# Transposing loads of ATT1 and Y3SP made in larger pieces, in a two-layer transformer kernel

## The reference

```python
x = layernorm(x + quat_attention(x))        # layer 0: 16 heads, full attention over 4096 tokens
x = layernorm(x + quantised_linear(x))      # blocks of 32 rounded to an fp6 grid, both operands
x = layernorm(x + window_attention(x))      # layer 1: q 16 heads, k and v 2 heads, window 256
                                            # out @ Wo + bo
xr = mu_r*x + (1-mu_r)*x_prev;  xk = mu_k*x + (1-mu_k)*x_prev     # x_prev: the token before
x = layernorm(x + sigmoid(xr @ W_r.T) * (relu(xk @ W_k.T)**2 @ W_v.T))
```

## Time and profile before

| | us |
|---|---|
| median of the runs shown (2 runs, 5682.71 to 5690.19) | 5686.45 |
| the profiled execution, its own time | 5682.38 |
| its span, from first to last instruction, slowest core (core 4) | 5680.8 |
| span of the fastest core (core 1) | 5646.2 |
| TensorE busy, share of the span | 2773.3 (49%) |
| ScalarE busy | 1807.1 (32%) |
| VectorE busy | 1534.1 (27%) |
| mean granted TensorE clock, share of full speed | 0.646 |

### The profile page before, as it was taken

How to read it: one execution, slowest core, us unless ns; L and a number is a source line. 1 busy time by engine, 2 the same in 40 slices (tenths; PEclk the granted TensorE clock), 3 DMA queues, 4 the chain that set the end, 5 groups by cost and what they waited for, 6 DMA issues and landing times.

```text
span 5680.8 us, 63040 instructions; the slowest of 8 cores (5646.2 to 5680.8 us)
## 1 busy us (share of the span) xinstructions
PE 2773.3 (49%) x17810; PEld 1397.2 (25%) x17810; DVE 1534.1 (27%) x3379; ACT 1807.1 (32%) x2292; POOL 177.8 (3%) x339
## 2 busy tenths in 40 slices
PE   0265257777775234555555555532445454104534
PEld 0122114444442122232323232311222222001112
DVE  0345310000001133413131313151333333013544
ACT  0122007778770133354444444410222222001000
POOL 0011010000001000000000000000000000000000
PEclk9966576666667555656666666666556555557766
DMA  1321230000003200000000000013000000101000
GB/s 15 75 36 28 45 45 4 4 1 4 4 4 48 52 12 20 13 10 16 10 16 11 16 11 16 11 28 70 25 27 22 25 25 27 40 20 27 18 30 23
DMA packets 200268, 132.74 MB, mean 23 GB/s; under 512 B 130152, under 2 KB 181008, under 8 KB 199952
## 3 DMA queue, kind: packets, MB, share of 16 engines
q0 software_dynamic: 46864, 59.31, 5.9%
q1 hardware_dynamic: 153088, 69.41, 4.4%
HBM read 117.63 MB, written 28.31 MB: 26 GB/s over the span
## 4 chain that ended last, share of the span: by engine, by line
PE 33%; ACT 22%; DVE 16%; DMA 9%; issue 9%; SPq 8%; POOL 1%; DVEq 1%; ACTq 1%; PEldq 0%; POOLq 0%
ACT TE L521 17%; PE PALL L551 9%; PE PALL L509 4%; SPq L1320 3%; PE PALL L464 3%; PE PALL L332 2%; SPq L1086 2%; PE PALL L1256 2%; PE PALL L1104 2%; PE PALL L797 2%; DMA TY<-XFF 2%; PE PALL L1188 1%; PE PALL L1463 1%; PE PALL L1403 1%; DMA SMALL<-QBI 1%
## 5 line engine op out<-in xcount | busy, mean ns | idle before, releaser
L521 ACT ACTIVATE TE<-PALL,BIASB 128x768 bf16<-128x768 f32 x1536 | 1383.5, 901 | 965.1 <-PE PALL L509 586.2
L509 PE MATMUL PALL<-TY 64*128 64x384 bf16 x3072 | 863.8, 423 | 697.7 <-ACT TE L521 685.8
L509 PEld LDWEIGHTS PALL<-TY 64*128 64x128 bf16 x3072 | 299.0, 97 | 1208.1 <-issue 1129.0
L551 PE MATMUL PALL<-TY,TE 128*128 128x65 bf16 x9216 | 530.5, 243 | 0.0
L551 PEld LDWEIGHTS PALL<-TY,TE 128*128 128x128 bf16 x9216 | 503.4, 131 | 60.3 <-issue 60.3
L558 DVE RECIPROCAL SMALL<-PALL 128x6 f32<-128x6 f32 x48 | 9.4, 196 | 1643.6 <-PE PALL L551 1617.0
L332 PE MATMUL PALL<-TY,TE 128*128 128x512 bf16 (+1 forms) x832 | 230.4, 450 | 362.1 <-DVE TE L298 210.9
L1232 ACT ACTIVATE TE<-PALL,BIASB 128x256 bf16<-128x256 f32 (+2 forms) x240 | 154.6, 644 | 464.5 <-PE PALL L1217 444.6
L464 PE MATMUL PALL<-TE,TY 128*128 128x512 bf16 x512 | 149.0, 444 | 239.8 <-DMA TY<-XFF 239.8
L1104 PE MATMUL PALL<-TE,TY 128*128 128x512 bf16 x288 | 102.9, 522 | 238.0 <-DMA TY<-ATT 236.9
L332 PEld LDWEIGHTS PALL<-TY,TE 128*128 128x128 bf16 x832 | 93.0, 114 | 499.3 <-issue 475.1
(11 more groups left out here) (171 smaller groups left out, 2628.1 us busy)
## 6 DMA issues: line engine op xcount, KB each, us to landing
TY<-XFF POOLq DMA_DIRECT2D x192, 128.0 KB, 4.7
TY<-XST POOLq DMA_DIRECT2D x18, 512.0 KB, 3.7
YOUT<-TE SPq DMA_DIRECT2D x18, 512.0 KB, 2.6
ATT<-TY SPq DMA_DIRECT2D x36, 128.0 KB, 1.8
TY<-ATT SPq DMA_TRANSPOSE x288, 2.3
Y2SP<-TY SPq DMA_DIRECT2D x18, 256.0 KB, 2.0
TE<-Y2SP POOLq DMA_DIRECT2D x18, 256.0 KB, 2.9
ATT<-TY SPq DMA_DIRECT2D x18, 256.0 KB, 2.3
```

What stands on the lines that cost most here:

```text
L509: t.matmul(o_, l_, r_, start=True, stop=True, tile_position=tp)),
L521: ss.activation(o_, i_, AF.Exp, bias=BIASB[:, 63:64], scale=0.125)),
L551: t.matmul(o_, l_, r_, start=s0, stop=False, skip_group_check=True)),
```

## The change

Two sets of transposing loads are issued in larger pieces. The same bytes go to the same engines.

1. `p4_slice` loads ATT1 by query tile: at slices 0, 3, 6, ... it issues 8 loads of 384 rows by 128 columns; the two slices after it read their part of the same buffer. The two `AF1` buffers grow from 2 KB to 6 KB per partition each, and the two `Y3B` buffers move behind them. The 18 sets of 8 loads become 6 sets of 8: 48 for 144.
2. The reload of Y3SP goes in five groups of 512, 512, 512, 512 and 256 rows: 40 loads for 144. Each group waits until the spills of its rows have landed, and for the group two before. What reads `Y3C` waits for the group that holds its columns.

```diff
@@ -1057,33 +1057,39 @@
         l_b1o = sch.dma("g", "dgm", lambda g: g.dma_start(out=ROWR[0:1, 0:1024], in_=B1O),
                         waits=[t_fbrow, tp2_nop, p2v_last])
 
-        def AF1(p, c):
-            base = p * 1024
-            return TY2.bitcast(BF16)[:, base + c * 128: base + c * 128 + 128]
+        def AF1(p, c, a, n):
+            base = p * 3072
+            return TY2.bitcast(BF16)[:, base + c * QT + a: base + c * QT + a + n]
 
         def Y3B(p):
-            return TY2.bitcast(BF16)[:, 2048 + p * 1024: 2048 + p * 1024 + 1024]
+            return TY2.bitcast(BF16)[:, 6144 + p * 1024: 6144 + p * 1024 + 1024]
 
         Z3AP = TEV(12288, F32, 1024)
         JUNK3 = TEV(16384, F32, 1024)
 
-        p4s = {"oproj": {}, "z3": {}, "spill": {}, "n": 0}
+        p4s = {"oproj": {}, "z3": {}, "spill": {}, "af1": {}, "n": 0}
 
         def p4_slice(sl):
             p = sl % 2
-            tldA = None
-            for c in range(8):
-                w = []
-                if c == 0:
-                    w = [("dsp", sch.cnt["dsp"])]
-                    if p4s["oproj"].get(sl - 2):
-                        w.append(p4s["oproj"][sl - 2])
-                    if sl < 2:
-                        w += [tp2_nop, p2v_last]
-                tldA = sch.dma("y", "dw2" if p == 0 else "dw3",
-                               (lambda y, s_=ATT1[128 * sl:128 * sl + 128,
-                                                  128 * c:128 * c + 128],
-                                d_=AF1(p, c): y.dma_start_transpose(d_, s_)), waits=w)
+            g = sl // 3
+            pg = g % 2
+            if sl % 3 == 0:
+                tldA = None
+                for c in range(8):
+                    w = []
+                    if c == 0:
+                        w = [("dsp", sch.cnt["dsp"])]
+                        if p4s["oproj"].get(3 * (g - 2) + 2):
+                            w.append(p4s["oproj"][3 * (g - 2) + 2])
+                        if g < 2:
+                            w += [tp2_nop, p2v_last]
+                    tldA = sch.dma("y", "dw2" if pg == 0 else "dw3",
+                                   (lambda y, s_=ATT1[QT * g:QT * g + QT,
+                                                      128 * c:128 * c + 128],
+                                    d_=AF1(pg, c, 0, QT): y.dma_start_transpose(d_, s_)),
+                                   waits=w)
+                p4s["af1"][g] = tldA
+            tldA = p4s["af1"][g]
             wy = [p4s["z3"][sl - 2]] if sl >= 2 else [("dy2", 16 * NSL), p2v_last]
             ldy2 = sch.dma("g", "dx0" if p == 0 else "dx1",
                            (lambda g, d_=TEV(20480 + p * 2048, BF16, 1024),
@@ -1099,7 +1105,7 @@
                         if psum_free.get(bank):
                             w.append(psum_free[bank])
                     sch.op("t", (lambda t, o_=PB(bank, 0, 512),
-                                 l_=AF1(p, ic),
+                                 l_=AF1(pg, ic, (sl % 3) * 128, 128),
                                  r_=TEV(24576, BF16, 8 * D)[:, ic * D + nh * 512: ic * D + nh * 512 + 512],
                                  s0=(ic == 0): t.matmul(o_, l_, r_, start=s0, stop=False)),
                            waits=w)
@@ -1304,21 +1310,21 @@
         tp3_nop = sch.op("t", lambda t: t.nop(), mark=True)
 
         zc = sch.op("v", lambda v: v.memset(SMALL[:, 166:167], 0.0))
-        rl_tok = {}
-        for sl in range(NSL):
-            dl = "dl0" if sl % 2 == 0 else "dl1"
+        RLG = [(0, 512), (512, 512), (1024, 512), (1536, 512), (2048, 256)]
+        rl_grp = {}
+        for gi, (a0, ng) in enumerate(RLG):
+            dl = "dl0" if gi % 2 == 0 else "dl1"
             tok = None
             for c in range(8):
                 w = []
                 if c == 0:
-                    w = [("dy3", 16 * (sl + 1)), tp3_nop, st1["pv_norm"]]
-                    if sl >= 2:
-                        w.append(rl_tok[sl - 2])
-                tok = sch.dma("y", dl, (lambda y, d_=Y3C(c, 128 * sl, 128),
-                                        s_=Y3SP[128 * sl:128 * sl + 128,
-                                                128 * c:128 * c + 128]:
+                    w = [("dy3", 16 * ((a0 + ng) // 128)), tp3_nop, st1["pv_norm"]]
+                    if gi >= 2:
+                        w.append(rl_grp[gi - 2])
+                tok = sch.dma("y", dl, (lambda y, d_=Y3C(c, a0, ng),
+                                        s_=Y3SP[a0:a0 + ng, 128 * c:128 * c + 128]:
                                         y.dma_start_transpose(d_, s_)), waits=w)
-            rl_tok[sl] = tok
+            rl_grp[gi] = tok
 
         if stage == "p4":
             for sl in range(NSL):
@@ -1346,16 +1352,14 @@
         TILES = [(0, 512), (512, 512), (1024, 512), (1536, 512), (2048, 256)]
 
         def rl_need(ti):
-            a, n = TILES[ti]
-            m = (a + n - 1) // 128
-            return [rl_tok[m], rl_tok[m - 1]]
+            return [rl_grp[ti]] + ([rl_grp[ti - 1]] if ti >= 1 else [])
         stash_tok = None
         for ti in range(1, 5):
             a = TILES[ti][0]
             for c in range(8):
                 stash_tok = sch.op("v", (lambda v, d_=SMALL[:, 96 + (ti - 1) * 8 + c: 97 + (ti - 1) * 8 + c],
                                          s_=Y3C(c, a - 1, 1): v.tensor_copy(d_, s_)),
-                                   waits=[rl_tok[(a - 1) // 128]] if c == 0 else [])
+                                   waits=[rl_grp[ti - 1]] if c == 0 else [])
         r_done = None
         xr_free = None
         for ti, (a, n) in enumerate(TILES):
```

## The result

The kernel after takes 5435.25 us (median of 9 runs, 5426.63 to 5464.16), the kernel before 5682.91 us beside it (8 runs). The ratio is 0.957, 95% interval 0.955 to 0.9591. The profiled execution took 5440.6 us; its slowest core is core 6.

A forecast was written before the change was run, and what follows sets the result against it. The prediction took SyncE's issuing of transposing loads as the bound. Savings of 125.0 us in the reload and 126.2 in the slices, 251 us together, took the median 5686.45 to 5435 us, range 5415 to 5462, chance 0.85.

The forecast's parts named there:

- SyncE's issues set both places: Reload and slices: the issue of transposing loads, not their transfer, is the limit; 1.290 us per issue in the reload.
- The price of an issue: Transposing loads: 1.262 us for 512 rows plus 0.058 us of gap, 1.32 us; eight of 384 rows 10.20 us.
- the hold-up: First group of the reload, beside the load of WRT: 8 us of delay, with 0.5 and 11.4 as ends.
- The bound that the prediction worked out for the first group: Reload's first group: 15.9 us of DMA work, begun 2 us in, so it lasts at most about 18 us.
- The spill distance: Slices: from one spill to the next, 6.3 us of VectorE's chain in place of a mean of 24.55.
- The rival of the clock: Second slice: TensorE does not get its upper clock level, 16 us of gain lost, 5451 us; chance 0.05.
- The slices as a whole: Slices: seven spill distances shorter by 18.25 us, 127.7 us, less 1.5 us for larger loads, saving 126.2 us.
- The reload was taken right: Reload: 40 issues, 52.8 us, plus 8 us of delay make 60.8 us for 185.8, saving 125.0 us.
- bytes, not issues: Reload and slices: a transposing load takes time in proportion to its rows; 5682 us, no change; chance 0.03.
- Contention that does not end with WRT: Reload: each of the five groups takes 21.98 us, the reload 110 us, the kernel 5484 us; chance 0.05.
- The slower rival: Large issues on the path, 88 of them: each held for 6.37 us, 5879 us, slower by 3.4%; chance 0.02.
- a later stage that grows: Sign of being wrong: a later stage grows, such as the feed-forward part, from L1367 to the end 601 us.

The follow-up runs named there:

- e1: The kernel before with only the reload of Y3SP made in groups of 512 rows, the slices loading ATT1 by 128 rows; 5557.55 us, ratio 0.9769.
- e2: The kernel before with only the slices loading ATT1 by 384 rows, the reload staying at 144 issues; 5580.6 us, ratio 0.9809.
- e4: The kernel after with the load of WRT held back until the last group of the reload has landed; 5437.97 us, ratio 0.9561.
- e3: The kernel after with the reload in nine groups of 256 rows, 72 issues for 40; 5479.52 us, ratio 0.9659.
- e5: The kernel after with the reload in three groups of 768 rows, 24 issues for 40; 5425.27 us, ratio 0.9527.

## Why the prediction was right

The forecast was 5435 us, and the measurement 5435.25. The gain was forecast at 251 us, from a kernel before at 5686.45; it is 247.7 us, from 5682.91 beside it. The mechanism holds, and the last few microseconds of agreement are luck, as said below. Its terms:

- That SyncE's issues set both places: e1 and e2 show it one by one, and the parts add up as the prediction took them to.
- The price of an issue by the earlier trace rows: 1.261 us for 512 rows and 10.18 us for eight of 384. The reload was to take 60.8 us and takes 60.71 on core 6, the first group 18 us and takes 18.9, the others 10.5 each and take 10.45. e4 shows that the cause of the hold-up is WRT, which the prediction could only take from one likeness, and 9 us for it from first to last issue on core 4.
- The size of the hold-up is a choice that came out well: 8 us, taken between 0.5 and 11.4. The bound that the prediction worked out for the first group, about 18 us from 11.8 us of weights and 4.1 us of transposes, did not hold: the first group takes 17.0 to 19.7 us on the eight cores, over 18 on four of them. In the 22 us from 4753 on core 6 the weight queue kept the engines busy for 61.5% of the time, 13.5 us, and the queue of the transposes for 37.1%, 8.2 us for 11 loads: side by side both took more of the engines than in the rows that the bound was taken from (a transposing load 0.75 us in place of 4.1 / 8 = 0.51).
- The spill distance: 6.3 us forecast, 6.37 measured, VectorE's chain as said. The rival of the clock is out: 1.90 us for eight matmuls in the second slice.
- The slices as a whole were taken 4 us too high: 126.2 forecast, 122.5 measured. Compared on core 6 in both kernels, the first two spills of a tile lie closer by 18.4 us, but the ATT1 loads of that tile and the next by only 17.5 (136.2 us apart, before 153.7). The stretch from the query load to the next ATT1 load got 0.8 us longer (104.7 for 103.9). Part of it is in the rows above: the query projection takes 12.84 us, and TensorE had stood 19.65 us before it. The same row of the kernel before, on core 6:

```profile
4093.55 12.28 PE L1188 MATMUL PALL<-TY 128*128 128x384 bf16 x64 [17.88 <-DMA TY<-Y2SP]
```

That the longer stand causes the slower start is what it looks like; no run varied it alone.
- The reload was taken right to 0.1 us in the stage table (125.0 forecast, 124.9 measured). So the exact total is luck: the 4 us too many in the slices are made up by the kernel before, which came out 3.5 us lower than the median that the forecast started from. Two figures of the prediction are off and change nothing: without hold-up the time is 5435 - 8 = 5427 us, not 5425, and with the price going by the bytes it is 5435 + 125 + 124 = 5684, not 5682.

The rival "bytes, not issues" falls with e3. "Contention that does not end with WRT" falls with the four later groups, 10.45 us each beside a DMA share of 0.40. The slower rival, every issue at 6.4 us, has its grain of truth: in every traced reload by 512 rows with WRT beside it the longest issue of each core takes 4.4 to 7.1 us, and in e4, with WRT held back, none takes over 1.27.

The rule that sequencer time is usually small relative to the DMA itself (the Trainium skill, DMA: Bandwidth & Descriptors, "Issuing engines are not separate DMA queues") would have had this change bring nothing. These runs disagree, with 1.23 us of SyncE for a load that keeps the DMA engines busy for 0.12 of that time.

The last stage of the kernel after is 3 us longer than before in the mean. The prediction had named a later stage that grows as a sign of being wrong (601 us from L1367 to the end); on core 6 that is 621.5 us, from 4817.47. It is cores 6 and 7 alone, at a lower granted clock; the windows of core 6 and of core 0 over it:

```profile
5000.00:5439.00 439.00, 201.80 (x772) 84.50 (x782) 211.25 (x396) 30.30 (x73) 0.00 (x0) 0.61 0.06 22
```

```profile
5000.00:5418.50 418.50, 176.60 (x772) 75.51 (x784) 211.28 (x396) 30.31 (x73) 0.00 (x0) 0.69 0.06 23
```

Core 6 had 427.7 us in this stage before, and 417.4 to 419.3 in all ten experiments, which have one or both parts of the change. In e4 it is cores 4 and 5 that are longer there (433.9 and 436.6). It is not the change; why the clock is lower on two cores of an execution stays open.

## What to carry to other kernels

Price a queue by its issues, not by its bytes: if a row of the same kernel shows the larger form of an issue, the sum can be made before anything is built, and here the reload came out right to 1 us and the slices to 4. Then ask what stands behind the issues in the same queue: 144 small loads cost 125 us more than 40 large ones when a 4 KB load, the border copies and with them a whole stage waited behind nearly all of them, and 49 us when they did not. And cut the time into stages before you read a difference of under 30 us in a total of 5,400.

## What the hardware showed that I had not expected

- The median issue of a transposing load grows by about 0.01 us for each 128 rows: 1.232, 1.242, 1.252, 1.262 and 1.280 us for 128 (before), 256 (e3), 384 (before), 512 (after) and 768 rows (e5) of 128 columns, on core 4. On the odd cores it is 0.03 us less throughout (1.202 for 128 rows, 1.230 for 512).
- Beside the load of WRT (8 loads of 256 KB) single issues of 512 rows take up to 7.1 us (e1) and of 768 rows up to 9.8 us (e5), while issues of 256 rows take at most 2.5 us (e3).
- MUK, a load of 4 KB, took 4.01 us in e4 on core 5, where WRT's first load was issued 0.11 us before it, and 1.53 us in the kernel after, where WRT had long landed.
